# Causal mask added in VectorE's row maximum, rotary sum on GpSimd, cosine product out of PSUM

## The reference

```python
x = x + 0.5 * ffn(layernorm(x))      # 16 experts, top 4, 64 hidden, plus a shared expert
x = x + attn(layernorm(x))
x = x + 0.5 * ffn(layernorm(x))

def attn(x, w_q, w_k, w_v):          # one head of 128, per batch of 1024 rows
    q, k, v = x @ w_q.T, x @ w_k.T, x @ w_v.T
    q, k = rotate(q), rotate(k)      # re = te*cos + to*sin; ro = -te*sin + to*cos
    scores = q @ k.T / sqrt(128)
    scores = where(lower triangle, scores, -inf)
    return softmax(scores) @ v
```

## Time and profile before

| | us |
|---|---|
| median of 3 runs | 991.23 |
| lowest and highest run | 986.24, 994.81 |
| span of the profiled execution | 993.2 |
| the six equal stretches, one per batch, from 419.39 to 586.65 | 27.85 to 27.89 each |

### The profile page before, as it was taken

The page is one execution under the profiler, slowest core; times in us unless marked ns, Lnnn a source line. Parts: engine busy times, 40 slices in busy tenths (PEclk is TensorE's granted clock), DMA queues, the critical chain, the costliest instruction groups (busy, mean ns, idle before and its releaser), DMA issues.

```text
span 993.2 us, 18642 instructions
## 1 busy us (share of the span) xinstructions
PE 891.7 (90%) x4608; PEld 723.0 (73%) x4608; DVE 863.8 (87%) x2309; ACT 582.7 (59%) x1189; POOL 529.1 (53%) x476
## 2 busy tenths in 40 slices
PE   2899999999999997799999999889999999989997
PEld 1577777767777765699988889767777777767775
DVE  5788999999989988788898888689989999999985
ACT  4466655566665554466666666656665556556664
POOL 4466666666666666322333231266665666665665
PEclk9999999999999999699999999999999999999999
DMA  8644543333444430000000000334455544443453
GB/s 241 185 99 112 118 99 86 86 86 87 96 110 109 110 88 1 1 1 2 1 0 0 0 0 1 87 87 99 111 122 119 120 104 96 96 96 98 108 120 82
DMA packets 52592, 81.08 MB, mean 82 GB/s; under 512 B 5328, under 2 KB 17488, under 8 KB 52304
## 3 DMA queue, kind: packets, MB, share of 16 engines
q1 hardware_dynamic: 52560, 80.71, 33.4%
HBM read 75.45 MB, written 5.24 MB: 81 GB/s over the span
## 4 chain that ended last, share of the span: by engine, by line
PE 20%; DVE 16%; issue 11%; DMA 9%; ACT 3%; SPq 1%; POOL 1%; DVEq 1%; ACTq 0%; POOLq 0%
PE bank L1049 15%; DMA qkT<-comb_rows 6%; DMA comb_rows<-combT 3%; PE bank L1239 2%; DVE probT L738 2%; PE bank L1199 2%; DVE comb L723 2%; DVE prob L730 1%; DVE chosen L703 1%; DVE rot L894 1%; DVE marked L698 1%; SPq L294 1%; DVE stats L746 1%; DVE rlogit L666 1%; DVE top L685 1%
## 5 line engine op out<-in xcount | busy, mean ns | idle before, releaser
L338 POOL TENSOR_TENSOR h_l<-probT,h_h 128x512 fp32r<-128x512 f32 x256 | 365.2, 1427 | 277.0 <-ACT h_h L423 272.9
L423 ACT ACTIVATE h_h<-probT 128x512 fp32r<-128x512 f32 (+1 forms) x288 | 181.3, 630 | 164.2 <-DVE probT L738 162.5
L730 DVE TENSOR_TENSOR prob<-prob,qkT 128x512 f32<-128x512 f32 x256 | 212.5, 830 | 46.7 <-DMA qkT<-comb_rows 25.0
L1049 PE MATMUL bank<-xh,w_h 128*128 128x512 f32 x544 | 230.8, 424 | 17.2 <-DVE probT L738 14.2
L1049 PE MATMUL bank<-xh,w_l 128*128 128x512 f32 x544 | 216.8, 399 | 0.0
L1049 PE MATMUL bank<-xl,w_h 128*128 128x512 f32 x544 | 216.2, 397 | 0.0
L459 ACT ACTIVATE prob<-bank 128x512 f32<-128x512 f32 (+1 forms) x288 | 169.9, 590 | 50.0 <-PE bank L1049 45.4
L738 DVE TENSOR_TENSOR probT<-prob,bank 128x512 f32<-128x512 f32 x256 | 172.0, 672 | 3.7
L1049 PEld LDWEIGHTS bank<-xh,w_h 128*128 128x128 f32 x544 | 103.5, 190 | 62.3 <-DVE probT L738 44.0
L1049 PEld LDWEIGHTS bank<-xh,w_l 128*128 128x128 f32 x544 | 103.4, 190 | 24.1
L1049 PE MATMUL bank<-h_h,w_h 128*128 128x512 f32 x288 | 116.9, 406 | 1.5 <-POOL h_l L338 1.1
(11 more groups left out here) (94 smaller groups left out, 1425.8 us busy)
## 6 DMA issues: line engine op xcount, KB each, us to landing
qkT<-comb_rows SPq DMA_DIRECT2D x256, 256.0 KB, 5.4
out_x<-X SPq DMA_DIRECT2D x16, 256.0 KB, 6.2
comb_rows<-combT SPq DMA_DIRECT2D x32, 32.0 KB, 1.8
cos<-in_cos SPq DMA_DIRECT2D x1, 1024.0 KB, 9.0
sin<-in_sin SPq DMA_DIRECT2D x1, 1024.0 KB, 10.9
qkv_both<-in_w13T SPq DMA_DIRECT2D x1, 832.0 KB, 4.7
qkv_both<-in_w2T SPq DMA_DIRECT2D x1, 576.0 KB, 7.3
X<-in_x SPq DMA_DIRECT2D x1, 512.0 KB, 6.3
```

Of the source, the lines that this page charges most:

```text
L338: nc.gpsimd.tensor_tensor(lo, f, hi.bitcast(F32), ALU.subtract).then_inc(done, 1)
L423: return nc.scalar.activation(dst, src, ACT.Copy)
L730: nc.vector.tensor_tensor(weighted[j % 2], silu[(q + j) % 2], comb_b[q][:, j, :], ALU.mult).then_inc(weighted_done, 1)
L1049: return nc.tensor.matmul(dst, lhsT, rhs, start=start, stop=stop)
```

## The change

Five things are changed.

1. The mask matmul in attn_scores is gone, and with it ident_r, the rounded mask and the ScalarE copies that made both. The mask is now plain float32 and 1152 columns wide: 1024 of zeros and then the triangle. A slice of it that starts at M - i * P is (i + 1) x 128 wide with the triangle at its end. It is loaded into its own tile.
2. attn_max is one instruction that adds the mask slice to the scores, multiplies by -1, writes the row back to the same place in PSUM, and takes the minimum of it, which is the negated maximum. attn_exp takes scale -1.
3. rope_add moves from VectorE to GpSimd, right behind rope_sin of the same block. It waits there for rope_c and rope_s of the block and for the buffer.
4. rope_c reads the projection from its PSUM bank instead of the SBUF copy (it still waits for the copy). So whoever takes that bank next waits for rope_c as well, and rope_c waits for rot of four blocks before.
5. In a step of VectorE, the wait for the scores and attn_rrow come before attn_max; attn_max has no waits of its own. Since attn_rrow(i) waits for exponential i, attn_max(i + 1) does too.

```diff
-        mask = sb("mask", [P, P], F32R)
-        ident_r = sb("ident_r", [P, P], F32R)
+        mask = sb("mask", [P, M + P])
...
-                    load(mask_f, mask_d, attn_loaded)
+                    load(mask[:], mask_d, attn_loaded)
...
+            def rope_add(b, n):
+
+                s = n % ROPE_BUFS
+                pool.wait_ge(rope_c_done, QB * b + n + 1)
+                pool.wait_ge(rope_s_done, QB * b + n + 1)
+
+                wait(pool, qkT_ready, QB // 2 * b + (n - ROPE_BUFS) // 2 + 1)
+                nc.gpsimd.tensor_tensor(rot[s][:], rope_c[s][:], rope_s[s][:], ALU.add).then_inc(rot_done, 1)
+
             def attn_prep(b, p, first=False):
 
                 for n in range(QB):
                     rope_sin(b, p, n)
+                    rope_add(b, n)
...
-                    copy(mask[:], mask_f).then_inc(consts_rounded, 1)
-                    copy(ident_r[:], ident[:]).then_inc(consts_rounded, 1)
...
-                                     ACT.Exp, bias=negmax[s][:],
+                                     ACT.Exp, bias=negmax[s][:], scale=-1.0,
...
                     dve.wait_ge(qkv_done, QB * b + n + 1)
-                    nc.vector.tensor_tensor(rope_c[s][:], qkv[p][:, n, 0:2 * D].rearrange("p (w d) -> p w d", w=2),
+                    wait(dve, rot_done, QB * b + n - ROPE_BUFS + 1)
+                    nc.vector.tensor_tensor(rope_c[s][:], bank[:, m, 0:2 * D].rearrange("p (w d) -> p w d", w=2),
                                             cos[:, n, :, :], ALU.mult).then_inc(rope_c_done, 1)
-                    if n >= 1:
-                        rope_add(b, n - 1)
                 else:
-                    if n == QB // 2 - 2:
-                        rope_add(b, QB - 1)
...
-                wait(dve, exp_done, QB * b + i - 1)
-                dve.wait_ge(scores_ready, QB * b + i + 1)
-                nc.vector.reduce_max(negmax[s][:], bank[:, 2 * s:2 * s + 2, :].rearrange("p a c -> p (a c)")[:, 0:w],
-                                     AX_X, negate=True).then_inc(negmax_done, 1)
+                row = bank[:, 2 * s:2 * s + 2, :].rearrange("p a c -> p (a c)")[:, 0:w]
+                nc.vector.tensor_tensor_reduce(row, row, mask[:, M - i * P:M + P], -1.0, 0.0 - MASKED, ALU.add, ALU.min,
+                                               negmax[s][:]).then_inc(negmax_done, 1)
...
+                    if i + 1 < QB or not last:
+                        dve.wait_ge(scores_ready, QB * b + i + 2)
+                    attn_rrow(b, p, i)
                     if i + 1 < QB:
                         attn_max(b, i + 1)
...
-                    attn_rrow(b, p, i)
...
                 elif kind2 == "qkv":
                     wait(pe, qkv_done, QB * row + n2 + 1)
+                    wait(pe, rope_c_done, QB * row + n2 + 1)
...
-                    diag = c == i // 4
-                    ins = mm3(dst, qkT_h[p][:, 0, qs], qkT_l[p][:, 0, qs], qkT_h[p][:, 1, k0:k1], qkT_l[p][:, 1, k0:k1],
-                              True, not diag)
-                    if diag:
-                        ins = mm(bank[:, 2 * s + c, k1 - k0 - P:k1 - k0], ident_r[:], mask[:], False, True)
+                    ins = mm3(dst, qkT_h[p][:, 0, qs], qkT_l[p][:, 0, qs], qkT_h[p][:, 1, k0:k1], qkT_l[p][:, 1, k0:k1])
...
                     if kind2 == "qkv":
                         pe.wait_ge(qkv_done, QB * (b + 1) + n2 + 1)
+                        pe.wait_ge(rope_c_done, QB * (b + 1) + n2 + 1)
...
+    mask = np.concatenate([np.zeros((P, M), np.float32), mask], axis=1)
```

More of the change, by code:

```diff
@@ L167, in macaron @@
         parts, at = {}, 0
-        for name, blocks in (("w13", 2 * UNITS - 1), ("w2", UNITS), ("wqkv", 3), ("mask", 1)):
+        for name, blocks in (("w13", 2 * UNITS - 1), ("w2", UNITS), ("wqkv", 3)):
             parts[name] = staged[:, at:at + blocks, :]
@@ L171, in macaron @@
         w13_f, w2_f = parts["w13"], parts["w2"]
-        wqkv_f, mask_f = (parts[n].rearrange("p n c -> p (n c)") for n in ("wqkv", "mask"))
+        wqkv_f = parts["wqkv"].rearrange("p n c -> p (n c)")
         x_loaded = [sem(f"x_loaded{n}") for n in range(3)]
@@ L184, in macaron @@
         wqkv_hi = sem("wqkv_hi")
-        consts_rounded = sem("consts_rounded")
         gw_split = sem("gw_split")
@@ L885, in ffn @@
                 residual(base + TILES - 1, TILES - 1)
-            def rope_add(b, n):
-                s = n % ROPE_BUFS
-                dve.wait_ge(rope_c_done, QB * b + n + 1)
-                dve.wait_ge(rope_s_done, QB * b + n + 1)
-                wait(dve, qkT_ready, QB // 2 * b + (n - ROPE_BUFS) // 2 + 1)
-                nc.vector.tensor_tensor(rot[s][:], rope_c[s][:], rope_s[s][:], ALU.add).then_inc(rot_done, 1)
             def attn_item(item, b, p, prologue=False):
@@ L1033, in _ @@
                 attn_item(item, 0, 0, True)
+            dve.wait_ge(scores_ready, 1)
             attn_max(0, 0)
@@ L1155, in ffn @@
                     pe.wait_ge(wqkv_split, 1)
-                    pe.wait_ge(consts_rounded, 2)
                 ffn_tile(T, 1, False, True, False, start)
```

## The result

| | before | after |
|---|---|---|
| median of five runs each | 993.94 | 998.69 |
| lowest and highest | 986.24, 994.81 | 996.74, 1003.57 |
| span of the profiled execution | 993.2 | 996.9 |

The ratio of the runs is 1.0073, 95% interval 1.0043 to 1.0104, which would be about 7.2 us. The two medians differ by 4.75 us only; with five runs each that spread over 7 to 9 us, neither number is exact, and both say that the kernel got slower by clearly less than 2%.

The account below looks back on a forecast made before the run. TensorE was taken as the limit for part of each batch and a loop over VectorE for a third of it; 7.0 - 0.8 + 0.3 = 6.5 us on the 993.2 span gave 999.7, median about 998, range 985 to 1010.

Parts of the forecast that it names:

- The bank waits: TensorE waits at three places per batch until VectorE's cosine product frees a projection bank: about 1.0 us per batch, 7 over seven.
- (a): TensorE's third projection of a batch waits for the cosine product on the first projection's bank: starts 0.65 us late.
- (b): TensorE's transposes qkT(0) need the bank of qkv(3), freed by its cosine product: 0.95 us late.
- (c): TensorE's second part of probT(4) needs the bank of qkv(6), freed by its cosine product: 1.5 us late.
- The order: Reciprocal before maximum on VectorE, so maximum i+1 waits for exponential i: nothing in loop batches, 0.3 us in the last.
- The first rival: VectorE, rid of the sums, reaches the product of qkv(6) earlier: kernel faster, 988 us, in the extreme 982; chance 0.3.
- The new maximum: VectorE's addition with minimum, written back to PSUM, replaces eight reductions per batch: taken as 0.1 us extra each.
- the second rival: The new maximum runs at half rate from reading and writing one PSUM row: 8 us over the batches, 1007 us; chance 0.25.
- The cosine product: VectorE's product reading PSUM instead of the SBUF copy: 0.43 us each time, without its long cases.
- The third rival: GpSimd becomes late: pairs of 1.95 us deliver rot(3) just as its transposes start, 0.2 us a batch, 1000 us; chance 0.08.
- Before batch 0: GpSimd's sums bring rstd about 1.6 us earlier, four instructions take 2.9 us instead of 2.2: 0.8 us gained.
- The last batch: The reduction over 1024 waits for the preceding exponential, delaying the routing weights and TensorE's transpose: 0.3 us later.

Follow-up runs that it names:

- their own run: Kernel before without the mask matmul and nothing in its place (diagonal blocks left unmasked): 990.97 us in one run, mean period 27.52 us.
- the run on block 6: Kernel after, with block 6 alone of each batch taking its cosine product from the SBUF copy: 998.63 us in one run, mean period 27.79 us.
- the mixed kernel: Kernel after, with the cosine product of blocks 0, 3 and 6 read from the SBUF copy, the others from the bank: 988.29 us, ratio to before 0.9942.
- the other last order: The mixed kernel, with the maximum of block i + 1 ahead of the reciprocal of block i in the last batch alone: 992.75 us, ratio to before 0.9980.
- 229: VectorE loop length of the kernel before with parts 1, 2 and 5 of the change: 997.85 us, ratio to before 1.0047.
- 230: VectorE loop length of the kernel before with eight tiny unused reciprocals added per batch: 1003.5 us.
- 222: VectorE loop length of the kernel before with four tiny unused reciprocals added per batch: 996.61 us in one run, mean period 27.89 us.
- both single-block kernels: Kernel after, with block 6 alone or block 0 alone taking its cosine product from the SBUF copy: 998.63 and 997.62 us, one run each.

## Why the prediction was right, step by step

**The forecast**, 998 us after a sum of +6.5, against a median of 998.69 and an attention of +6.7. The closeness of the two times is partly luck: 998 started from a median of 991.23 over three runs, which became 993.94 over five, and the span, forecast at 999.7, was 996.9 because the feed-forwards came out 3 us shorter in that trace. What the prediction is to be held to is the attention. Its mechanism is the one that decided, and the runs separate it from the rivals.

**The bank waits.** (a) 0.65 forecast; without the wait of block 0 the leg to (a) is 0.54 shorter (the period 0.68). That this leg came out as forecast, 16.68 against 16.63, has a second error in it: the masks on it give 0.25 back by their own run, not 0.45. (a) to (b) 0.30 forecast, 0.30 measured; the terms that the prediction wrote down for this leg add to 3.72, not to 3.75 to 3.85, and it booked the upper end, which is what was measured. (b) to (c) 0.55 forecast, 0.34 measured: VectorE reached the product of block 6 at 482.55, 7.68 us after (b), where the prediction's own times (483.4, and 502.39 + 0.95 less a period) put 7.95. All told +0.97 per period against +1.0. The signs named ahead were there too: VectorE at 20 us busy, GpSimd at 13.2 (forecast 14), no wait of TensorE on rot. The order was put at nothing in the loop batches, because the exponential would be long over. Alone it costs 0.16 us a period, and in the kernel after VectorE stands up to 0.86 us for it:

```profile
484.93 0.16 DVE L921 RECIPROCAL rrow<-rowsum 128x1 f32<-128x1 f32 x1 [0.86 <-ACT prob L556]
```

Whether that lengthens the period there too was not tried.

**The first rival** (VectorE gets ahead) failed for the reason given against it. VectorE did stand idle for 9 us a period, but ahead of (c) it had to wait for ScalarE's copy of qkT(1) (0.84 us, until 479.98), and then had qkT_l, statistics, maximum and residual to do, which ended at 482.6 and not at 482.0. The gaps of an engine are no help if they lie ahead of the input that the queued work waits for. With no wait at (c) at all, the run on block 6 gives a period of 27.79: about the old time, no gain.

**The new maximum.** Groups of the kernel after (ns minimum, median, maximum): 

```profile
L916 DVE DVE_READ_ACCUMULATOR2_ANT negmax<- x64: 136/141/147, 406.4 to 628.9; 128x1 f32 x64
...
L904 DVE TENSOR_TENSOR rope_c<-bank,cos x64: 406/424/426, 387.2 to 598.1; 128x256 f32<-128x256 f32 x64
...
L408 POOL TENSOR_TENSOR rot<-rope_c,rope_s x64: 723/732/743, 390.4 to 599.8; 128x256 f32<-128x256 f32 x64
...
L397 POOL TENSOR_TENSOR rope_s<-qkv_both,sin x64: 723/736/746, 389.5 to 599.0; 128x256 f32<-128x256 f32 x64
```

Over 768 columns it takes 0.95 us as above, over 1024 1.23 (the reduction: 0.94 and 1.21). The read of the accumulator is a second instruction of 0.14 us, but the residual starts in the same instant, at 482.29. So the extra is nearly 0, not 0.1, and the second rival is out: reading and writing one PSUM row kept the rate of the plain reduction.

**The cosine product** took 0.42 us each time, as forecast. What I had not priced is that GpSimd gained as well: 0.73 us every time, where it had a median of 0.89 and up to 0.98. The median falls to 0.73 with either the source or the sum changed alone; only with both are the long cases gone (at most 0.75, against 0.98 to 1.0). The third rival never showed, but with the bank waits gone it is rot that TensorE waits for, 2.7 us between 450 and 560 us. The Trainium skill (SBUF — State Buffer, Who interferes with whom) says that a VectorE instruction with at most one SBUF input, outside the modes that use both ports, doesn't contend with GpSimd. Here the trace agrees, and the mixed kernel shows both cases in one program: 409 to 427 ns from the bank, up to 1171 from the copy. The Trainium skill's fixed cost of a PSUM source (VectorE: DVE Perf Modes, the TRN2 errata; 120 cycles against 58, by estimate 65 ns more) is not seen: the median is 424 ns from the bank, against 414 for the two-input sum of the same shape.

**Before batch 0**: forecast 0.8 us gained; by TensorE's first transposes behind the last sum 0.2 (from the first rope_s 14.36 us, before 14.58). GpSimd in the kernel after:

```profile
399.00 1.65 POOL L389 TENSOR_TENSOR rstd<-var_eps,neg_half 128x8 f32<-128x8 f32 x1
400.62 0.73 POOL L397 TENSOR_TENSOR rope_s<-qkv_both,sin 128x256 f32<-128x256 f32 x1
401.48 0.72 POOL L408 TENSOR_TENSOR rot<-rope_c,rope_s 128x256 f32<-128x256 f32 x1
402.16 0.72 POOL L397 TENSOR_TENSOR rope_s<-qkv_both,sin 128x256 f32<-128x256 f32 x1
403.01 0.72 POOL L408 TENSOR_TENSOR rot<-rope_c,rope_s 128x256 f32<-128x256 f32 x1
```

rstd ended 1.3 us earlier (forecast 1.6), but the four instructions and the handover then took 3.26 us where two and VectorE's sums had taken 2.16. From a rope_s to the sum that waits for it is 0.86, from a sum to the next rope_s 0.68: I had left out what it costs when the sum waits for the result of the instruction just before it.

**The last batch**: forecast +0.3, measured +1.0. ScalarE and VectorE of the kernel after, answering to the earlier trace rows:

```profile
626.50 1.01 ACT L556 ACTIVATE prob<-bank,negmax 128x896 f32<-128x896 f32 x1
...
629.22 1.12 ACT L556 ACTIVATE prob<-bank,negmax 128x1024 f32<-128x1024 f32 x1
```

```profile
627.70 0.17 DVE L921 RECIPROCAL rrow<-rowsum 128x1 f32<-128x1 f32 x1 [1.38 <-ACT prob L556]
627.78 1.23 DVE L916 CUSTOM_DVE_ANT_0 bank<-bank,mask 128x1024 f32<-128x1024 f32 x1
...
630.16 0.28 DVE L729 SCALAR_TENSOR_TENSOR comb<-wsel,rsum 128x64 f32<-128x64 f32 x1
```

The step was drawn correctly: the maximum waits for exponential 6, the last exponential is no later for it (2.72 us after exponential 6, before 2.70), the routing weights are. From exponential 6 to the comb_rows DMA went 5.15 us (626.50 to 631.65) where 4.87 had gone: the 0.3 of the forecast. Of the 1.0, 0.5 is the place of the cut: from the exponential over 1024 columns of batch 6 the last stretch grew from 24.50 to 24.98 only. So 0.2 is lost between that exponential and exponential 6, where I looked at nothing. By the same cut the order alone lengthens this stretch by 0.63 and its removal from the mixed kernel shortens it by 0.59; the sum alone and the bank source alone leave it as it was (24.49 and 24.50). So the order is enough to explain what the last batch lost.

**Batch 0**: a seventh microsecond was booked for it. From TensorE's first transposes behind the last sum to the exponential over 1024 columns it took 29.71 us, before 29.07. So 0.4 was booked too much there, 0.6 too little before batch 0, 0.2 too little in the last batch and 0.2 too much over the six periods: these nearly cancel, and the sum came closer than its terms deserve. These ends are not exact either: up to its maximum the attention took 40.11 us in the mixed kernel and 40.93 with the other last order, which is the same program there, so 0.8 of scatter lies on this stretch.

**The mask's load** stayed hidden. The sine table landed 0.9 us later after its issue (11.8 against 10.9), and ScalarE's first copy of the attention's weights starts when it did:

```profile
51.72 0.51 ACT L431 ACTIVATE wqkv_h<-qkv_both 128x384 fp32r<-128x384 f32 x1
```

## What to carry to other kernels

When a consumer is changed to read a buffer at its source instead of a copy, the buffer is taken until that consumer's turn comes. What counted here is the work queued in front of it on its engine at the moment when the copy would have been done, not how busy the engine is. The remedy was selective: let the instances whose buffer is asked for at once keep the copy, and the others read the source. And price a removed piece of work together with its partner: taking the sums from VectorE alone brought 0.05 us a period, taking the masks from TensorE alone 0.36, both (with the new maximum and its order) 0.53. And choose the event at which a trace is cut on an engine whose place in the loop the change doesn't move, or cut at two.

## What the runs showed of the hardware

- **VectorE's longer loops loaded their code anew on each turn.** With 229 and 230 instructions there were seven packets on q14 in 100 us, and VectorE stood for up to 2.2 us at a time; with 214, 217 and 222 there was no such cost. Length and place in memory are not separated. The profile shows it only as idle time released by "issue", together with a queue of kind "instruction" in the middle of a loop.
- **The feed-forward tile has two lengths**, whatever the attention does. SyncE's comb_rows issues in the kernel after:

```profile
181.28 0.48 SPq L286 DMA_DIRECT2D comb_rows<-combT  x1
...
202.44 0.48 SPq L286 DMA_DIRECT2D comb_rows<-combT  x1
...
224.81 0.48 SPq L286 DMA_DIRECT2D comb_rows<-combT  x1
```

One tile took 21.16 us, the next 22.37. Of the 28 distances behind the first of each stage, 2 were of the short kind in the trace before and 5 in the trace after, 9 in the kernel before with the bank source, 1 in the mixed kernel and none in the mixed kernel with the old last order. Three more short ones are 3.5 us, and the two feed-forwards together are 3.4 us shorter in the trace after than before (665.3 against 668.7 from first to last issue): that accounts for the span's 3.7 us where the attention has 6.7. The last two kernels differ by 2.8 us in the same sum (668.5 and 671.3) at equal attentions, half of the 5.7 us between their spans. What picks the length was not tried. The counts go as much with the chip that a trace was taken on as with the kernel: 6, 9, 4 and 3 short ones in the four kernels on one, 1, 5, 3 and 0 on the second, 0, 0, 0 and 2 on the third, where both single-block kernels ran. A single span of this kernel is not to be trusted to 3 us.
- **A GpSimd instruction that waits for the one before it** starts 0.18 us later than one that doesn't (0.86 against 0.68 from start to start, for 0.72 us of work).
- **Arithmetic in place in PSUM with a second input from SBUF** ran at the rate of a plain reduction: 1.23 us over 1024 columns, 0.55 over 384 (the reduction: 1.22 and 0.55).
